# Turning seven tiles by VectorE's block flips and a DRAM scratch in place of TensorE transposes, three half tiles in flight

## What is computed

```
x = x + layernorm(attention(layernorm(x)))    # 16 heads of 16, causal, LoRA on qkv and on the projection
x = x + layernorm(ffn(layernorm(x)))
ffn: h = x; for blk in 0..2:
    y = linear(h, dequantized W[2 blk] + LoRA) + bias
    y = gelu(layernorm(y) * gamma + beta)
    h = linear(y, dequantized W[2 blk + 1] + LoRA) + bias + h
```

## Time and profile before

| | before |
|---|---|
| median of 3 runs | 1291.52 us |
| the profiled execution | 1291.09 us |
| its span | 1289.3 us |
| TensorE busy | 1237.8 us (96%) |
| ScalarE busy | 1108.9 us (86%) |
| VectorE busy | 767.8 us (60%) |
| GpSimd busy | 402.8 us (31%) |
| mean granted TensorE clock | 0.989 |

### The profile page before, as it was taken

One profiled execution on the slowest core, in us unless ns is written; L12 is line 12 of the kernel. 1 busy time (PEld: TensorE's weight loads), 2 busy tenths in 40 slices (PEclk: granted clock), 3 DMA queues, 4 the chain that ended last, 5 costly groups with the idle time before them and its releaser, 6 DMA issues.

```text
span 1289.3 us, 30421 instructions
## 1 busy us (share of the span) xinstructions
PE 1237.8 (96%) x11653; PEld 550.9 (43%) x11653; DVE 767.8 (60%) x1825; ACT 1108.9 (86%) x1263; POOL 402.8 (31%) x1397
## 2 busy tenths in 40 slices
PE   8999999999999999999999999999999999999866
PEld 6556434444434443444443343333433334333345
DVE  6775226677554664767566554565553575663576
ACT  4665999899999999998999989999998999989533
POOL 3221235333432234223423233231531224231153
PEclk9999999999999999999999999999999999999979
DMA  5985643433422323232322222232422222220000
GB/s 172 312 305 178 181 120 116 122 92 116 124 70 88 103 83 120 89 96 83 107 88 87 64 92 86 67 101 67 134 84 71 66 80 91 70 67 6 22 1 17
DMA packets 68049, 130.13 MB, mean 101 GB/s; under 512 B 14502, under 2 KB 29884, under 8 KB 67900
## 3 DMA queue, kind: packets, MB, share of 16 engines
q1 hardware_dynamic: 63612, 123.88, 30.7%
q10 hardware_dynamic: 4288, 4.26, 1.1%
HBM read 102.94 MB, written 20.97 MB: 96 GB/s over the span
## 4 chain that ended last, share of the span: by engine, by line
PE 72%; DVE 7%; ACT 6%; issue 4%; POOL 1%; DMA 0%; ACTq 0%; DVEq 0%
PE O L1403 32%; PE S L1385 22%; PE F L209 15%; ACT probs L1328 6%; DVE feed_mem L1600 2%; DVE feed_mem L1601 1%; PE F L1454 1%; PE S L1473 1%; DVE stC L1495 1%; DVE feed_mem L1529 0%; DVE feed_mem L1590 0%; DVE tmpC L1513 0%; DVE feed_mem L1599 0%; PE S L1458 0%; PE S L1471 0%
## 5 line engine op out<-in xcount | busy, mean ns | idle before, releaser
L1328 ACT ACTIVATE probs<-S 128x1024 f32<-128x1024 f32 x1056 | 998.6, 1031 | 72.9 <-PE S L1385 53.1
L1403 PE MATMUL O<-probs,vg 128*32 128x512 f32 (+3 forms) x4608 | 523.7, 564 | 0.8 <-DVE o_turned L1552 0.7
L1385 PE MATMUL S<-q_op,k_op 64*128 64x512 f32 (+3 forms) x2304 | 375.7, 421 | 16.7 <-ACT probs L1328 14.8
L1385 PEld LDWEIGHTS S<-q_op,k_op 64*128 64x128 f32 x2304 | 184.8, 185 | 284.8 <-ACT probs L1328 199.8
L1403 PEld LDWEIGHTS O<-probs,vg 128*32 128x32 f32 x4608 | 117.7, 109 | 202.5 <-issue 189.8
L1280 POOL TENSOR_SCALAR tmpC<-mvC 128x2 f32<-128x2 f32 x84 | 19.4, 231 | 460.4 <-DVE rstdC L1505 459.1
L1307 POOL TENSOR_SCALAR_AFFINE_SELECT probs<-probs 128x512 f32<-128x512 f32 (+1 forms) x160 | 97.7, 618 | 179.6 <-ACT probs L1328 179.3
L1529 DVE TENSOR_SCALAR feed_mem<-feed_mem,rstdC,nmrC 128x256 f32<-128x256 f32 x168 | 76.9, 499 | 114.7 <-POOL nmrC L1291 109.7
L1584 DVE TENSOR_TENSOR feed_mem<-F,bffn 128x512 f32<-128x512 f32 x56 | 38.5, 687 | 135.2 <-PE F L209 135.0
L209 PE MATMUL F<-wfT,feed_mem 128*32 128x256 f32 x1792 | 117.5, 380 | 0.5 <-DVE feed_mem L1603 0.4
L1600 DVE SCALAR_TENSOR_TENSOR feed_mem<-feed_mem 128x512 f32<-128x512 f32 x126 | 103.1, 818 | 7.9 <-DVE feed_mem L1590 5.0
(11 more groups left out here) (183 smaller groups left out, 1049.8 us busy)
## 6 DMA issues: line engine op xcount, KB each, us to landing
k_op<-qk_rows SPq DMA_DIRECT2D x256, 256.0 KB, 3.6
qk_rows<-parts SPq DMA_DIRECT2D x32, 512.0 KB, 4.5
q_op<-qk_rows SPq DMA_DIRECT2D x128, 128.0 KB, 2.9
k_op<-qk_rows SPq DMA_DIRECT2D x48, 128.0 KB, 2.6
x_in<-in_L_attn_x ACTq DMA_DIRECT2D x8, 512.0 KB, 5.0
feed_mem<-in_L_attn_x SPq DMA_DIRECT2D x16, 256.0 KB, 3.4
attT<-o_div SPq DMA_DIRECT2D x126, 32.0 KB, 2.1
out<-feed_mem SPq DMA_DIRECT2D x14, 256.0 KB, 2.9
```

What stands on the lines that cost most here:

```text
L1328: nc.scalar.activation(probs[:, n % NP, :, :], S[:, n % NS, :, :], ACT.Exp, scale=SCALE).then_inc(exp_ok, 1)
L1385: last = nc.tensor.matmul(S[:, n % NS, a, at:at + TT - q0], k_op[mine, c % RING, pair, k0:k0 + P], q_op[mine, v % QS, pair, q0:TT], start= ...
L1403: last = nc.tensor.matmul(O[h * STRIP:(h + 1) * STRIP, q0:TT], vg[:, kb, col:col + STRIP], probs[:, n % NP, a, at:at + TT - q0], start=fir ...
```

## The change

For tiles 0 to 6 the steps turn_x, turn0, turn1 and turn2 leave TensorE's list (`FEED_STEPS`). In their place stand four parts: the norm writes its rows so that, for each 32 channels, both blocks of 128 tokens stand side by side; VectorE flips all 32x32 blocks of the half in one instruction of 128x512 (flip); SP writes the result to a DRAM scratch `turns` with four DMAs of 64 KB, one for each 32 partitions, each in 256 runs of 64 values, 256 bytes (put); and SP reads it back with one DMA of 256 KB, channels on the partitions, in rows of 1 KB (get). The get of x lands in hT directly, so copy_x goes for these tiles; the other gets land in zT, and VectorE scales them in place by gamma and beta. The token order inside a half is permuted by this, and the products read their stationary operand in the matching order (`rows_of`).

The buffers are now per lane: three lanes, half number 2t + k in lane (2t + k) mod 3, the third lane's buffers in `qkv_mem`. A half's projection waits for the result of the half three before it, no longer for the previous tile's last step. The planned copy time falls from 0.95 to 0.9 us and the norm's rises from 0.8 to 0.95. The due times go from 50 to 62 blocks per tile. Tile 7 keeps its transposes on TensorE and uses the places of lanes 0 and 1. The core of the diff, with the semaphores by lane, the helpers `own`, `own_t`, `slots` and `place_in` (which pick a half's buffer), and the renamed arguments left out:

```
+FEED_STEPS = [x for x in STEPS if not x.startswith("turn")]
...
-FEED_FROM, FEED_EACH = 24.0, 50.0
+FEED_FROM, FEED_EACH = 24.0, 62.0
...
+TURNS = ["_x"] + [str(m) for m in range(BLK)]
+PUTS, GETS = [f"put{x}" for x in TURNS], [f"get{x}" for x in TURNS]
+LANDING.update({x: 2.4 for x in PUTS + GETS})
...
+LANES = 3
...
+def half_before(t, k, n):
+    j = 2 * t + k - n
+    return (j // 2, j % 2) if j >= 0 else None
+def lane(t, k):
+    return (0, LANES, 1, LANES + 1)[k] if t == NT - 1 else (2 * t + k) % LANES
+def steps(t):
+    return STEPS if t == NT - 1 else FEED_STEPS
...
-             ("norm_x", 0.8, 0.6, ("rs_x",)), ("copy_x", 0.8, 0.45, ("turn_x",))]
+             ("norm_x", 0.95, 0.6, ("rs_x",)), ("flip_x", 0.75, 0.0, ("norm_x",)), ("put_x", 2.8, 0.0, ("flip_x",)), ("get_x", 0.7, 0.0, ("put_x",))]
...
-                  (f"norm{m}", 0.8, 0.6, (f"rs{m}",)), (f"copy{m}", 0.95, 0.45, (f"turn{m}",)), (f"sq{m}", 0.72, 0.0, (f"copy{m}",)),
+                  (f"norm{m}", 0.95, 0.6, (f"rs{m}",)), (f"flip{m}", 0.75, 0.0, (f"norm{m}",)), (f"put{m}", 2.8, 0.0, (f"flip{m}",)),
+                  (f"get{m}", 0.7, 0.0, (f"put{m}",)), (f"copy{m}", 0.9, 0.0, (f"get{m}",)), (f"sq{m}", 0.72, 0.0, (f"copy{m}",)),
...
+    return "get_x" if name == "first0" and t < NT - 1 else FEEDS[name]
...
-        mine = [(name, t, k, n) for name in STEPS for k in range(parted(t)) for n in range(pieces(name, t))]
+        mine = [(name, t, k, n) for name in steps(t) for k in range(parted(t)) for n in range(pieces(name, t))]
...
-            found = [(ENDING, t - 1, k, pieces(ENDING, t - 1) - 1)] if 0 < t < NT - 1 else [("evac_fold", FOLDS - 1, 0)] if not t else []
+            prior = half_before(t, k, LANES) if t < NT - 1 else None
+            found = [] if t == NT - 1 else [("result",) + prior] if prior else [("evac_fold", FOLDS - 1, 0)]
...
+        flat = [[g["feed_mem"][:, (2 * n + s) * EACH:(2 * n + s + 1) * EACH] for s in range(2)] + [g["qkv_mem"][:, n * EACH:(n + 1) * EACH]] for n in range(4)]
+        zT, hT = ([m.rearrange("p (c t) -> p c t", c=NC) for m in flat[n]] for n in range(2))
+        u, y = ([m.rearrange("p (b c) -> p b c", c=C) for m in flat[n]] for n in range(2, 4))
+        uT, yT = ([m.rearrange("p (c t) -> p c t", c=NC) for m in flat[n]] for n in range(2, 4))
...
+                    elif x[0] in PUTS:
+                        inputs_done(sp, *x)
+                        s = lane_of(x)
+                        for i in range(P // STRIP):
+                            sp.dma_start(d["turns"][s].rearrange("(j e) (i r) -> e j i r", e=STRIP, i=P // STRIP)[:, :, i, :],
+                                         flat[2][s][i * STRIP:(i + 1) * STRIP, :].rearrange("e (j r) -> e j r", j=C // STRIP)).then_inc(put_ok[s], 16)
+                    elif x[0] in GETS:
+                        inputs_done(sp, *x)
+                        s = lane_of(x)
+                        sp.dma_start((hT if x[0] == "get_x" else zT)[s][:, :, :], d["turns"][s].rearrange("(c p) n -> p c n", p=P)).then_inc(got_ok[s], 16)
...
+                        rows_of = lambda m, c: m[:, c, tok] if name == "project" or t == NT - 1 else m[:, c, :].rearrange("p (i b r) -> p b i r", i=P // STRIP, r=STRIP)[:, j]
...
+                    if name == "evac_att" and prior:
+                        part_done(dve, "result", *prior)
...
-                    elif name == "copy_x":
-                        emptied(t, k, nc.vector.tensor_copy(hT[:, :, toks(t, k)], in_channels(name, t, k)))
+                        emptied(t, s, nc.vector.tensor_tensor(own(u, t, k), in_rows(name, t, k), col.unsqueeze(1).to_broadcast([P, nb, C]), ALU.add))
+                    elif name.startswith("flip"):
+                        nc.vector.transpose(flat[2][s][:, :], flat[3][s][:, :]).then_inc(dve_ok[s], 1)
                     elif name.startswith("copy"):
+                        z = own_t(zT, t, k)
                         for c in range(NC):
                             col = m * NC + c
-                            last = nc.vector.tensor_scalar(zT[:, c, toks(t, k)], in_channels(name, t, k)[:, c, :], halved[:, col:col + 1],
+                            last = nc.vector.tensor_scalar(z[:, c, :], z[:, c, :], halved[:, col:col + 1],
                                                            halved[:, BLK * NC + col:BLK * NC + col + 1], ALU.mult, ALU.add)
-                        emptied(t, k, last)
+                        last.then_inc(dve_ok[s], 1)
...
-                        scaled(t, k, xt if name == "norm_x" else u).then_inc(dve_ok[k], 1)
+                        src = xt if name == "norm_x" else own(u, t, k)
+                        for j in range(nb):
+                            row = slots(t, k).start + j
+                            last = nc.vector.tensor_scalar(flat[3][s].rearrange("p (i b r) -> p b i r", b=nb, r=STRIP)[:, j], src[:, j, :].rearrange("p (i r) -> p i r", r=STRIP),
+                                                           rstd[:, row:row + 1], nmr[:, row:row + 1], ALU.mult, ALU.add)
+                        last.then_inc(dve_ok[s], 1)
...
+    d["turns"] = nc.dram_tensor("turns", [LANES, C, HT], F32).ap()
```

More of the change, by code:

```diff
@@ L205, in strips @@
 def strips(matmul, out, lhsT, rhs, **how):
-    for p in range(0, P, STRIP):
-        last = matmul(out[p:p + STRIP], lhsT[:, p:p + STRIP], rhs, **how)
+    for n in range(P // STRIP):
+        last = matmul(out[n * STRIP:(n + 1) * STRIP], lhsT[:, n, :] if len(lhsT.shape) == 3 else lhsT[:, n * STRIP:(n + 1) * STRIP], rhs, **how)
     return last
@@ L1206, in inputs_done, with stored_before @@
                     part_done(eng, a, t, k)
+        def stored_before(eng, t, k):
+            s, _, _ = place_in(t, k)
+            many = sum(lane(*x) == s for x in halves if (x[0] < NT - 1 if t == NT - 1 else x < (t, k)))
+            if many:
+                eng.wait_ge(stored[s], 16 * many)
         def move(eng, v, heads):
@@ L1219, in normed @@
         def normed(name, t, k):
-            return in_rows(name, t, k) if t == NT - 1 else u[:, rows(t, k), :]
+            return in_rows(name, t, k) if t == NT - 1 else own(u, t, k)
         with nc.Block() as block:
```

262 lines of the change are left out of this document (142 added, 120 removed).

## The result

The changed kernel takes 1270.9 us (median of 4 runs, 1269.5 to 1273.2) against 1291.5 for the kernel before on the same chip: ratio 0.985, 95% interval 0.9838 to 0.9862, 20.6 us less. The profiled execution took 1270.7 us for a span of 1269.0, so it stands for the median. The forecast was 1262.5, 29.0 us less than before. The kernel is faster, as said, but 8.4 us of the forecast gain are missing.

A forecast was written before the change was run, and what follows sets the result against it. TensorE was taken to lead ScalarE in the attention stretch. Removing 33.0 us of turns, less 4.8 given back at the end, gains 28.2 us: 1291.5 to 1263, stated as 1262.5, range 1252 to 1276 (0.54).

The forecast's parts named there:

- the signs that the prediction named for its mechanism: Attention stretch: length near 1065 us, ScalarE's product waits 30 to 35, TensorE's exponential waits up, feed ending 20 to 40 ahead.
- arrive in full: Attention stretch: all 33.0 us of removed TensorE turns shorten the time, being less than ScalarE's 62.9 us of waits.
- rival D: Attention stretch: many turns stand where ScalarE is full and TensorE's time free; 17.4 us arrive, 1279 us; chance 0.10.
- VectorE's flips: VectorE in the attention stretch: 56 flips of 0.711 us add 39.8 us, hidden because VectorE mostly waits for others.
- the forecast of 25 to 30 more: Attention stretch: VectorE's busy time was to rise by 25 to 30 us.
- The queues and the turn's route: SP's queue and DMA: flip 0.71, issues 1.75, put landing 3.0, get landing 3.4; sum 8.9 us, range 8.0 to 11.5.
- 4.8 us given back: End of the attention: feed finishes some 28 us early, so TensorE's spare 17% there finds no work, losing 4.8 us.
- 22 us of longer turns: Feed of each half: four turns, each 5.7 us longer, less a copy, lengthen 160 us to 182 (178 to 192).
- ten handoffs late by half a microsecond: Attention stretch: late gets, some 5 us, set against a gain from more evenly spread feed; both taken as nothing.
- A, late gets: TensorE's fixed order stalls on late gets: 56 handoffs of 0.8 us, 45 us lost, 1308 us; chance 0.14.
- B, lanes too slow: Feed of the halves: from 195 us per half it ends after the attention could, giving 1276 to 1289; chance 0.08.
- C, evenness: Attention stretch: three halves fill thin stretches, removing half of ScalarE's remaining 30 us of wait, 1243 us; chance 0.12.

The follow-up runs named there:

- idle_turns: Changed kernel plus four unread identity transposes on TensorE directly ahead of each product that needs a turned input, tiles 0 to 6: 1303.1 us, ratio 1.0106.
- due66: Changed kernel with the planner spreading each tile's feed over 66 blocks instead of 62: 1267.1 us, ratio 0.9825.
- margin64: Changed kernel with 64 blocks per tile and the planned landing of each put and get raised from 2.4 to 3.5 us: 1261.6 us, ratio 0.9781.
- margin62: Changed kernel, still 62 blocks per tile, with only the planned landing of puts and gets raised from 2.4 to 3.5 us: 1267.2 us, ratio 0.9816.
- pe_turns_3lanes: Changed kernel keeping three lanes and due times, but with TensorE transposes again for tiles 0 to 6, no flips, puts or gets: 1288.8 us, ratio 0.9988.
- puts_twice: Changed kernel with each put issued twice, first to a spare scratch, the get waiting for both: 1325.6 us, ratio 1.0282.
- real64_late: Changed kernel planned with measured put and get prices, 64 blocks per tile, tile 6's feed due between blocks 411 and 520: 1284.9 us, ratio 0.9949.

## Why the prediction was right, and where 8 us went

The time lies in the forecast range, which was 24 us wide, and TensorE's removed work is what moved it: without the flips the other parts bring 1.7 us. Several of the signs that the prediction named for its mechanism failed, though. The stretch is 1077 us long and not near 1065, ScalarE waits 57.6 us and not 30 to 35, TensorE's wait for exponentials went down and not up, and the feed ends 60 us ahead and not 20 to 40. In the stretch alone 12 us are missing: the exponentials end 16.3 us sooner than before (1195.8 against 1212.1), where 28.2 were forecast. The other 4 us of the 20.6 come from behind the stretch, where the prediction had no gain. That part is luck.

**What bounds the kernel, and the 33.0 us.** TensorE leads before and after: right. That the 33.0 us "arrive in full" is not shown. idle_turns has 32 to 33 of 33 arriving, but for time directly ahead of the feed's products. The turns stood elsewhere, nearly all of them in runs of exponentials without a wait. That is rival D's mechanism, with TensorE's time free there. Its 17.4 us are close to the 17.8 to 18.9 that the flips moved by themselves, but only if nothing else was lost: with the losses below taken off, 17.4 leaves 4 and 33.0 leaves 20. So most of the 33.0 arriving fits the sum better, and D's mechanism in part is not excluded. No run decides it.

**VectorE's flips.** Right: 0.71 each, 39.6 us, and hidden but for a few microseconds at most, as another 40 us cost 6. In the second line of the windows VectorE is busy 633.07 us, no more than in the earlier trace rows: the forecast of 25 to 30 more failed, at no cost to the time. The group of copies (9.6 us) went as forecast; the scaling fell from 41.5 us to 21.9 + 8.8, at 0.408 us from SBUF where it took 0.536 from PSUM, and no gain was taken for that. The rest is mostly in the polynomial, 17 us less. One of its lines in the kernel before, then after; count, then least, median and longest time in ns (the 36 others of after, into `qkv_mem`, have the same median):

```profile
L1600 DVE SCALAR_TENSOR_TENSOR feed_mem<-feed_mem x126: 642/692/1579, 228.0 to 1201.3; 128x512 f32<-128x512 f32 x126
```
```profile
L1697 DVE SCALAR_TENSOR_TENSOR feed_mem<-feed_mem x90: 642/692/1112, 247.9 to 1119.5; 128x512 f32<-128x512 f32 x90
```

The median is the same, 0.69 us; only the mean fell, from 0.82 to 0.71. In both traces no such instruction that runs without a GpSimd instruction beside it takes over 0.70 us. In the kernel before, 27 of 126 took more than 0.8, all beside GpSimd's triangle cut or square; after, 7 of 126 did. So fewer of them met these GpSimd instructions, or were held up when they did. Which, and why, was not tried.

**The queues and the turn's route.** The sum was short, 8.9 us where the 56 turns took 10.7 on the mean. Its terms were a little high: issue 0.46 for a put and not 0.58, landing 2.3 for the last put and 3.3 for the get, not 3.0 and 3.4, together 7.8. What it left out is the standing in SP's queue, 1.1 us ahead of the puts and 1.9 ahead of the get (2.6 in the turn shown, 458.4 less 455.8), which the prediction named and did not put into the sum.

The Trainium skill, "VectorE: DVE Perf Modes", The three transpose paths, holds a plain DMA that transposes by strides to be 19 times slower than the crossbar when the innermost stride at the destination is large. The prediction left that condition out. The puts write runs of 64 neighbouring values, so the rule does not speak of them, and no run here has a DMA of which it does. They land in 1.9 us for 64 KB (median), against 2.0 us for the moves of 32 KB in rows of 2 KB.

**The half's length and the end.** This is the step that failed most clearly: the term "4.8 us given back", for 28 us without feed. The first half of tile 6 took 158 us from projection (969.8) to store (1127.6), not 182, and the second was through 8 us after it, not 20. Its projection began 17 us later than forecast, and the exponentials ended 13 us later. Together the feed was through 60 us before the last exponential (1135.5 and 1195.8) and not 28. The forecast added 22 us of longer turns to the 160 us that a half took before; but this half took no longer than one did then, so part of the 160 was waiting that the longer turns could fill. (That is read from the two lengths and was not tested.) By the prediction's own rate, 2.39 us of TensorE per three exponentials, 71 of them need 56.6 of 65.7 us: an estimated 9.1 us given back, 4.3 more than forecast.

**Late gets, taken at nothing.** The stall near 900 us costs about 4 us (worked out from its rows). The prediction set "ten handoffs late by half a microsecond" against a gain from evenness and took zero for both. ScalarE's wait of 57.6 us, not 30 to 35, shows no gain from evenness. Together 4.3 + 4 = 8.3, against 8.4 missing. The runs have losses of this size, but do not assign them: due66, which shortens the end and leaves the gets, brings 3 to 4 us; margin64, with the same end and room for the gets, brings 5.5 more; margin62, with that room and an end that shrank by itself, only about 4.

The match of 8.3 and 8.4 is chance. In the stretch 12 us are missing and these two terms explain 8 of them; the shorter tail hides the rest. Against pe_turns_3lanes 33.0 less 9.1 less 4 is 20, and 17.8 to 18.9 was measured. The tail behind the last exponential also became 4.0 us shorter (73.2 us from its end to the end of the span, against 77.2), which the prediction had as unchanged. It is as short, 73.0, with three lanes and TensorE's turns, so it comes from the lanes or the due times; which, stays open. And orders that differ in a planner's constant alone scatter by some microseconds (margin62 and margin64 by 5.6) for reasons that single stalls explain only in part. What the rest of the missing gain is, and whether the 33.0 were there to begin with, stays open.

**The rivals.** A, late gets, did not happen in the size that it names, but puts_twice puts it at most 2 us away. Its threshold of 0.5 us of mean stall on TensorE looked at the wrong engine: TensorE's direct waits for the scratch stayed at 15 us there while 55 were lost. B, lanes too slow, is what two lanes show. C, evenness, did not come: ScalarE's wait for scores is 45.5 us even in margin64, which takes 1261.6 where C had 1243. D, turns in stretches where TensorE's time is free, is not excluded, as said above. The run that could decide it, idle transposes at the places where the turns stood, was not made.

## What to carry to other kernels

Where the order is fixed at build time, the price that the planner has for a step is also its insurance. Here the fastest order reckoned a DMA route, on a queue that it shares, at 3.4 us above its measured price, and the slowest but one at 0.1 above; try a price above the median before the median itself. When work is taken from the leading engine, ask what fills that engine's time at the end of the stretch; a chain that finishes early leaves time that nothing can use, and one that finishes late holds up the next stage, so both ends have to be swept (50, 62, 66 and 70 blocks gave 1273.9, 1270.9, 1267.1 and 1270.1). To price a suspected saving, put the removed work back as idle work, but at the place where it stood: on an engine that is ahead in some stretches and behind in others, the same 0.6 us cost everything at one place and perhaps nothing at another.

## What the runs showed of the hardware

Writes of 256-byte runs were cheap. The profile's row of q1 rose from 63612 packets and 30.7% of 16 engines to 139772 and 40.9%: 76160 packets for (0.409 x 1269.0 - 0.307 x 1289.3) x 16 = 1970 us of engine time, 0.026 us each, where the prediction allowed 0.1. By the packets of that trace, one of 256 bytes takes 0.019 us on the mean and one of 1 KB 0.053, so a byte costs 1.4 times as much in the shorter runs. The Trainium skill, "DMA: Bandwidth & Descriptors", Specifications, wants 512 bytes or more for the line rate and has a read-modify-write below. No run here tells such a step apart; the dearer byte is all that these packets show.

TensorE's clock turns a short stall into a longer one. After 0.55 and 2.41 us of idle time close together the granted clock was 0.50, 1.2 GHz, in the 4 us from 904, and 32 weighings took 4.49 us, where 16 took 1.92 a little later. The same happened after 4.95 us of waiting for the flipped O in real64_late: the granted clock was 0.50 in the 4 us from 258, and eight weighings took 1.93 us and not 1.06.

A VectorE instruction can take more than twice as long beside a GpSimd one. Of the 126 instructions of L1600 in the kernel before, the 89 without overlap took at most 0.69 us, and the longest beside GpSimd 1.58.
